# A language-model block in eight token blocks: where the FFN weights are split and turned, and in what order block 0 is attended

## What is computed

```python
h = rms_norm(rms_norm(emb[x], norm_weight) @ proj.T)            # [16*256, 512]
n = layernorm(h)
q, k = feature_map(n @ Wq.T) / sqrt(32), feature_map(n @ Wk.T)   # per head, width 32
attn = tril(q @ k.T) ** 2
h = h + ((attn @ (n @ Wv.T)) / (attn.sum(-1) + eps)) @ Wo.T
y = fwht(layernorm(h) * SU_ug)                                   # 512 wide
u = silu(y @ W_gate.T * s_g) * (y @ W_up.T * s_u)                # 2048 wide
out = h + (fwht(u * SU_dp) @ W_down.T) * s_d
```

## Time and profile before

| | us |
|---|---|
| time, median of 3 runs | 1403.45 (1400.7 to 1405.17) |
| the profiled execution | 1400.2 |
| its span in the trace | 1398.4 |
| prologue, to the first FFN matmul | 162.75 |
| block 0, gate and up slots | 154.75 |
| block 0, down slots | 55.0 |
| rest (block 1 to the end) | 1025.9 |

### The profile page before, as it was taken

One profiled execution on the slowest core, in us unless ns is written; L12 is line 12 of the kernel. 1 busy time (PEld: TensorE's weight loads), 2 busy tenths in 40 slices (PEclk: granted clock), 3 DMA queues, 4 the chain that ended last, 5 costly groups with the idle time before them and its releaser, 6 DMA issues.

```text
span 1398.4 us, 19203 instructions
## 1 busy us (share of the span) xinstructions
PE 1306.7 (93%) x7481; PEld 643.6 (46%) x7481; DVE 532.3 (38%) x1049; ACT 398.7 (29%) x703; POOL 422.9 (30%) x371
## 2 busy tenths in 40 slices
PE   5575598989999999999999999999999999999999
PEld 3352255554444444444444444444444444444444
DVE  1655567654422253226222432234222523251110
ACT  4453463440233113321233023311322123211220
POOL 0342143332144313432244213421433124321210
PEclk9888699999999999999999999999999999999999
DMA  8911100002100130003000210012001300020000
GB/s 297 288 27 23 24 1 9 8 8 54 53 8 9 31 75 8 15 15 80 19 16 8 68 38 8 15 42 64 8 8 23 83 8 15 15 68 23 0 0 30
DMA packets 101681, 55.73 MB, mean 40 GB/s; under 512 B 74180, under 2 KB 90872, under 8 KB 101112
## 3 DMA queue, kind: packets, MB, share of 16 engines
q1 hardware_dynamic: 98112, 45.77, 12.8%
q0 software_dynamic: 2560, 8.39, 2.0%
q10 hardware_dynamic: 952, 0.75, 0.2%
HBM read 29.47 MB, written 8.65 MB: 27 GB/s over the span
## 4 chain that ended last, share of the span: by engine, by line
PE 83%; DVE 6%; DMA 4%; ACT 4%; issue 2%; POOL 1%; SPq 0%; DVEq 0%; ACTq 0%
PE bank L1078 24%; PE bank L1079 24%; PE bank L1080 23%; DMA prod<-sg 3%; PE bank L1231 3%; PE bank L1073 2%; PE bank L1216 2%; PE bank L1215 2%; PE bank L1121 1%; DMA hid<-in_L_tok_norm_weight 1%; PE bank L1240 1%; ACT xT L855 1%; DVE wgu L477 1%; PE bank L1071 1%; ACT wgu L855 1%
## 5 line engine op out<-in xcount | busy, mean ns | idle before, releaser
L1078 PE MATMUL bank<-xT,wgu 128*128 128x512 f16 x1024 | 389.3, 380 | 1.4 <-DVE xT L708 1.4
L1079 PE MATMUL bank<-xT,wgu 128*128 128x512 f16 x1024 | 389.3, 380 | 0.0
L1080 PE MATMUL bank<-xT,wgu 128*128 128x512 f16 x1024 | 389.2, 380 | 0.0
L398 POOL TENSOR_TENSOR hid<-a,hid 128x512 f16<-128x512 f32 x128 | 147.9, 1156 | 512.0 <-ACT hid L855 512.0
L743 DVE SCALAR_TENSOR_TENSOR a<-bank,kap,sg 128x512 f32<-128x512 f32 x128 | 96.0, 750 | 477.5 <-PE bank L1080 324.4
L1078 PE MATMUL bank<-wd,hid 128*128 128x512 f16 x512 | 194.3, 379 | 0.0
L1079 PE MATMUL bank<-wd,hid 128*128 128x512 f16 x512 | 194.1, 379 | 0.0
L1080 PE MATMUL bank<-wd,hid 128*128 128x512 f16 x512 | 194.0, 379 | 0.0
L358 POOL TENSOR_TENSOR p<-prod,p 128x512 f16<-128x512 f32 x128 | 153.2, 1199 | 128.4 <-ACT p L855 128.4
L855 ACT ACTIVATE hid<-a 128x512 f16<-128x512 f32 x128 | 80.6, 630 | 279.5 <-DVE a L743 279.5
L1080 PEld LDWEIGHTS bank<-xT,wgu 128*128 128x128 f16 x1024 | 100.4, 98 | 121.6 <-issue 1.4
(11 more groups left out here) (178 smaller groups left out, 1245.8 us busy)
## 6 DMA issues: line engine op xcount, KB each, us to landing
out<-a SPq DMA_DIRECT2D x24, 256.0 KB, 2.2
wgu<-in_L_ffn_W_gate SPq DMA_DIRECT2D x16, 256.0 KB, 5.5
wgu<-in_L_ffn_W_up SPq DMA_DIRECT2D x16, 256.0 KB, 5.0
wd<-in_L_ffn_W_down SPq DMA_DIRECT2D x4, 1024.0 KB, 9.4
ids_b<-in_x SPq DMA_DIRECT2D x8, 256.0 KB, 3.5
out<-h_row SPq DMA_DIRECT2D x8, 256.0 KB, 2.0
xT<-in_L_tok_proj_weight SPq DMA_DIRECT2D x1, 1024.0 KB, 8.6
p<-in_L_attn_Wq SPq DMA_DIRECT2D x1, 1024.0 KB, 13.8
```

The costliest lines, as they stand in the source:

```text
L398: nc.gpsimd.tensor_tensor(hid[:, 1, s, :], a32[:, :], hid[:, 0, s, :], ALU.subtract)\
L1078: mm(dst, w[0], v[0], start=first, stop=False)
L1079: mm(dst, w[0], v[1], start=False, stop=False)
L1080: return mm(dst, w[1], v[0], start=False, stop=final)
```

## The change

1. **Loads.** The load of the norm weight is issued before that of the projection instead of after it. A group of four gate or up units comes with one DMA of 2 KB rows instead of four; the tile `wgu` has another layout.
2. **Gate and up units.** 12 units (0 to 11) are turned on PE in slots 1 to 12 of block 0's attention, with one diagonal per unit. The other 20 are prepared in slots 0 to 9 of block 0's FFN, two per slot, without PE: ACT scales the unit in place, ACT writes the f16 high part to a staging buffer (L966, twice), POOL the low part (L428), and SP turns the pair with a DMA transpose (L329) into `wgu`. There are three staging buffers (`RING`), taken in turn; the next user waits for the landing.
3. **W_down.** The 16 butterflies are two per slot in slots 2 to 9 (L566, L567). A unit is then split in SBUF (ACT L966, DVE L556), three per slot in slots 10 to 14 and one in slot 15, turned by a DMA transpose through the same three buffers, and multiplied with the f16 Hadamard matrix in the slot after (two f16 matmuls, L1256 and L1257: after the gate half, after the up half and after the attention step), then evicted (ACT L966, DVE L574).
4. **Block 0's attention** has 18 slots. The count and the W_v turns come earlier, the squares of W_o and of the units move between the slots, the low parts of `att` are made between the first products, and `p` alternates between two tiles. W_o is turned in slots 13 to 16. `oT` and `xT` are turned by PE (eight f16 transposes into a bank) and copied by one ACT instruction of 128x1024. The W_o rows are no longer slots but a `tail()`, in which bound, norm and scale steps stand between the rows on DVE.
5. **Banks.** Block 0's gate half alternates between two banks in slots 0 to 7; the up half has one.

Its core (lines of `...` are left out):

```diff
@@ -19,19 +19,18 @@
...
-BEFORE = 16
-UNITS_IN_SLOT = (0, 0) + (1,) * BEFORE + (0,) * 14
-UNITS_BESIDE = 16
-NORM_AT = {4: 1, 24: 2}
-SCALE_AT = {6: 1, 26: 2}
-DIAG_AT = {6: (2,), 10: (3,), 26: (4,), 27: (5,)}
-BOUND_AT = 17
-NORM_BESIDE, SCALE_BESIDE = 2, 3
-DIAG_BESIDE = {3: (6,), 5: (7,)}
-BOUND_BESIDE, FIT_BESIDE = 4, 5
+RING = 3
+TURNED = 12
+UNIT_AT = tuple(range(1, 13))
+UNITS_BESIDE = 10
+SQUARES_AT = {j: (3, j) for j in range(4)} | {8 + j: (4 + j // 4, j % 4) for j in range(8)}
+WO_SQUARES_AT = (4, 5, 6, 7)
+WO_UNIT_AT = (13, 14, 15, 16)
+DOWN_SQUARES = (3, 3, 3, 3, 2, 2)
+BOUND_BESIDE, FIT_BESIDE = 1, 6
+MIX_BESIDE = (2, 2, 3, 3, 4, 4, 5, 5, 6, 6, 7, 7, 8, 8, 9, 9)
+SPLIT_BESIDE = (10, 10, 10, 11, 11, 11, 12, 12, 12, 13, 13, 13, 14, 14, 14, 15)
 DOWN_ORDER = (3, 2, 0, 1)
-MIXED_BEFORE = 2
-MIX_BESIDE = (1, 2, 3, 4, 5, 6, 7, 8, 9, 10, 11, 12, 12, 13)
...
+HEADS_AT0 = (4, 8, 12, 16)
+O_AT0 = (5, 9, 13, 16)
+O_FLIP_AT0 = (6, 10, 14, 17)
+SLOTS0 = 18
...
+def down_third(s, i):
+    return down_splits(s - 1)[i:i + 1]
...
-        GATE0, UP0, D_TURN, D_HADA = banks[0], banks[1], banks[2], banks[3]
+        GATE0, UP0, D_HADA = [banks[0], banks[1]] * 4 + [banks[0]] * 8, banks[2], [banks[3], banks[1]]
...
             nc.sync.dma_start(late[:, 1536:1792], c_square).then_inc(S["c_land"], 16)
+            nc.sync.dma_start(nw_b, rows(norm_w, D)).then_inc(S["nw_land"], 16)
             nc.sync.dma_start(small_raw[0], quarters(proj_w)).then_inc(S["p_land"], 16)
-            nc.sync.dma_start(nw_b, rows(norm_w, D)).then_inc(S["nw_land"], 16)
...
                 w, g = (w_up if n % 2 else w_gate), n // 2
-                for i in range(4):
-                    rows_of_tile = w[512 * g + P * i:512 * g + P * i + P, :].rearrange("p (k d) -> p k d", k=DC)
-                    nc.sync.dma_start(raw[n][:, :, i, :], rows_of_tile).then_inc(S[f"gu_land{n}"], 16)
+                rows_of_tile = w[512 * g:512 * g + 512, :].rearrange("(i p) d -> p i d", p=P)
+                nc.sync.dma_start(raw[n], rows_of_tile).then_inc(S[f"gu_land{n}"], 16)
...
+            def unit_turn(x):
+                if x < UNITS:
+                    sp.wait_ge(S["st_low"], x - TURNED + 1)
+                else:
+                    sp.wait_ge(S["st_lo"], x - UNITS + TURNED + 1)
+                nc.sync.dma_start_transpose(unit_home(x), stage_of(x).rearrange("p l d -> p (l d)"))\
+                    .then_inc(turning(x), 16)
...
+                for x in units_beside(s) + [UNITS + v for v in down_splits(s)]:
+                    unit_turn(x)
+                if s in SUMS_AT:
+                    o_turn(1, SUMS_AT.index(s))
...
+            def unit_low(x):
+                pool.wait_ge(S["st_hi"], x + 1)
+                nc.gpsimd.tensor_tensor(stage_of(x)[:, 1, :], unit_raw(x), stage_of(x)[:, 0, :], ALU.subtract)\
+                    .then_inc(S["st_low"], 1)
...
             for s in range(SLOTS):
                 feed(0, s)
+                for x in units_beside(s):
+                    unit_low(x)
                 product(1, s)
...
+            def unit_low(x):
+                dve.wait_ge(S["st_hi"], x + 1)
...
+                else:
+                    nc.vector.scalar_tensor_tensor(stage_of(x)[:, 1, :], unit_raw(x), unit_scale(x), stage_of(x)[:, 0, :],
+                                                   ALU.mult, ALU.subtract).then_inc(S["st_lo"], 1)
...
+            def tail():
+                for m in range(4):
+                    row_sum(0, m)
+                    if m:
+                        x_low(0, m - 1)
+                    if m > 1:
+                        xT_low(0, m - 2)
+                    row_norm(0, m)
+                    if m == 0:
+                        pair_norm(2)
+                        half_terms(0)
+                    if m == 1:
+                        pair_scale(2)
+                        bound_low(0)
+                    if m == 2:
+                        half_scale(0)
+                    if m == 3:
+                        pair_norm(3)
+                xT_low(0, 2)
+                x_low(0, 3)
+                xT_low(0, 3)
+                pair_scale(3)
...
-                for u in units_beside(2 * s):
-                    unit(u, D_TURN)
-                for v in down_evicts(2 * s):
-                    down_unit(v)
                 feed(0, s, UP0)
-                for u in units_beside(2 * s + 1):
-                    unit(u, D_TURN)
-                for v in down_evicts(2 * s + 1):
+                for v in down_splits(s):
+                    unit_low(UNITS + v)
...
+                for v in down_third(s, 2):
+                    down_unit(v)
...
+            def unit_high(x):
+                if x < TURNED:
+                    n, i = unit_place(x)
+                    act.wait_ge(S["turned"], x + 1)
+                    copy(wgu[:, n, i, 0, :, :].rearrange("p k f -> p (k f)"), TURN[x % 3][:, :]).then_inc(S["st_hi"], 1)
+                    return
+                if x >= TURNED + RING:
+                    act.wait_ge(*landed(x - RING))
+                else:
+                    act.wait_ge(S["wo_ready"], 1)
+                if x < UNITS:
+                    act.wait_ge(S["gu_scaled"], x // 8 + 1)
+                    copy(unit_raw(x), unit_raw(x), scale=unit_scale(x)).then_inc(S["st_scaled"], 1)
+                    act.wait_ge(S["st_scaled"], x - TURNED + 1)
+                    copy(stage_of(x)[:, 0, :], unit_raw(x)).then_inc(S["st_hi"], 1)
+                else:
+                    act.wait_ge(S["d_mix"], 4 * ((x - UNITS) // 4) + 4)
+                    act.wait_ge(S["bound_done"], 1)
+                    copy(stage_of(x)[:, 0, :], unit_raw(x), scale=unit_scale(x)).then_inc(S["st_hi"], 1)
...
-            def down_turn(v):
-                dt, fq = DOWN_ORDER[v // 4], v % 4
+            def down_hada(v):
+                if v > 1:
+                    pe.wait_ge(S["d_lo"], v - 1)
                 if v == 0:
-                    pe.wait_ge(S["d_diag"], 1)
-                    pe.wait_ge(S["w_lo"], UNITS)
-                else:
-                    pe.wait_ge(S["d_copied"], v)
-                pe.wait_ge(S["d_mix"], 4 * (v // 4) + 4)
-                turn(D_TURN, lambda i: WD[dt][:, (4 * fq + i) * P:(4 * fq + i + 1) * P],
-                     lambda i: d_diag[:, dt, :], S["d_turned"])
-
-            def down_hada(v):
-                pe.wait_ge(S["d_copied"], v + 1)
-                if v:
-                    pe.wait_ge(S["d_lo"], v)
-                else:
                     pe.wait_ge(S["bound_low"], 3)
-                mm(D_HADA[:, :], hada, wt[:, v % 2, :], start=True, stop=True).then_inc(S["d_hada"], 1)
-
+                pe.wait_ge(*landed(UNITS + v))
+                w = wd[:, DOWN_ORDER[v // 4], v % 4, :, :, :].rearrange("p l f d -> p l (f d)")
+                mm(D_HADA[v % 2][:, :], hada16[:, :], w[:, 0, :], start=True, stop=False)
+                mm(D_HADA[v % 2][:, :], hada16[:, :], w[:, 1, :], start=False, stop=True).then_inc(S["d_hada"], 1)
...
+            def tail():
+                wo_rows(0, 0)
+                wo_rows(0, 1)
+                wo_rows(0, 2)
+                x_flip(0)
+                wo_rows(0, 3)
+                bound_sum(0)
+                for m in range(4):
+                    x_mix(0, m)
+                    if m < 3:
+                        x_flip(m + 1)
 
 
...
             for s in range(SLOTS):
                 if s < FT:
                     if s == 0:
                         pe.wait_ge(S["xT_done"], 4)
-                        pe.wait_ge(S["w_lo"], BEFORE)
-                        pe.wait_ge(S["bound_low"], 1)
-                    else:
-                        pe.wait_ge(S["silu_done"], s)
-                    if s % 4 == 0:
-                        pe.wait_ge(S["w_lo"], min(UNITS, 8 * (s // 4) + 8))
-                    feed_half(s, 0, GATE0, S["gate_ready"])
-                    for v in down_evicts(2 * s):
+                        pe.wait_ge(S["wo_lo"], 4)
+                    if s >= 2:
+                        pe.wait_ge(S["silu_done"], s - 1 if s < 9 else s)
+                    pe.wait_ge(*landed(2 * s))
+                    feed_half(s, 0, GATE0[s], S["gate_ready"])
+                    for v in down_third(s, 0):
                         down_hada(v)
-                    for u in units_beside(2 * s):
-                        turn_beside(u)
-                    for v in down_turns(2 * s):
-                        down_turn(v)
                     if s == BOUND_BESIDE + 1:
                         bound_sum(1)
                     if s == FIT_BESIDE + 1:
                         bound_sum(2)
                     if s:
                         pe.wait_ge(S["a_done"], s)
+                    pe.wait_ge(*landed(2 * s + 1))
                     feed_half(s, 1, UP0, S["up_ready"])
-                    for v in down_evicts(2 * s + 1):
+                    for v in down_third(s, 1):
                         down_hada(v)
```

(22 more changed lines are left out.)

790 lines of the change are left out of this document (428 added, 362 removed).

## The result

The changed kernel takes 1409.58 us (median; 1407.02 to 1410.50), the kernel before 1403.11 in the same comparison. The ratio is 1.0046 with a 95% interval of 1.0036 to 1.0056: slower by 6.5 us. The forecast was 1412, slower as well, within a range of 1378 to 1427. The profiled execution has a span of 1406.5 us, 8.1 more than before.

A forecast was written before the change was run, and what follows sets the result against it. A chain over all engines was taken to bound the prologue, PE the FFN slots. 1400.2 - 10.7 (prologue) + 19.2 (block 0's gate and up slots) = 1408.7 us profiled, 1412 on the median's scale; range 1378 to 1427.

The forecast's parts named there:

- First head sums: Prologue: the first head sums start at 63.4 us instead of 80.06, a gain of 16.7 us.
- the order of the loads: Start of the prologue: norm weight loaded before the projection gains 1.3 us, bounds 0 and a few us.
- the tail: End of the prologue, the W_o rows: 41 us instead of 36.10, a loss of 4.9 (bounds 34 and 45).
- both stalls: Tail: DVE waits at `bound_low(0)` for a PE sum and at `pair_norm(3)` for ACT's squares, 3 to 4 us each.
- The mechanism: Block 0 FFN, slots 2 to 9: DVE's butterflies and POOL's instructions take turns, 9.05 us a slot.
- a sign of being wrong: Block 0 FFN, slots 2 to 9: slots under 8 us would show the forecast wrong; it expected 9 us.
- the buffers as a rival: Three staging buffers make ACT wait for landings, deciding from 4.4 us a transpose: 1425 to 1435 us; with more lock, chance 0.11.
- The chain: Block 0 FFN, slots 11 to 15: one chain through every engine, 11.4 us a slot, 13.3 with half rate.
- half rate: Slots 11 to 15: PE at half rate for some 4 us after idling costs 1.9 us more per slot.
- the case that came: Whole kernel: slower by 5 to 16 us, 1408 to 1420 us, chance 0.45.
- the faster rival: Block 0 FFN: preparation hides, gate and up slots take 130 to 150 us, total 1375 to 1398; chance 0.30.
- The preparation hides: Block 0 FFN: turns cost less than taken, slots 2 to 9 take 6.4 to 7 us, total 1375 to 1398; chance 0.30.

The follow-up runs named there:

- e6: Changed kernel with the norm weight's load issued behind the projection's again: 1408.9 us, ratio to the kernel before 1.0049.
- e7: Changed kernel with the tail's bound_low(0), half_scale(0) and pair_norm(3) one step later on DVE: 1404.9 us, ratio to the kernel before 1.0026.
- e2: Changed kernel with each W_down butterfly made on one eighth of its columns, the rest left out: 1388.5 us, ratio to the kernel before 0.9890.
- e8: Changed kernel with the same 16 butterflies spread, one per slot in slots 2 to 9, two in 10 to 13: 1395.2 us, ratio to before 0.9953.
- e3: Changed kernel with DVE's first two W_down evictions of a slot before the three splits: 1396.4 us, ratio to the kernel before 0.9941.
- the combined kernel: Changed kernel with fourth staging buffer, evictions before splits, butterflies spread, tail's bound and norm steps a row later: 1375.0 us, ratio to before 0.9810.
- e1: Changed kernel with a fourth staging buffer for the gate and up units: 1405.6 us, ratio to the kernel before 1.0007.

## Why the prediction was right

**Prologue.** First head sums and first W_o matmul came within 1 us of the forecast. The 1.3 us for the order of the loads stay unproven (e6): the chain waits for the projection until 12.1 us, where before it waited for the norm weight until 12.3. The term that was mis-sized is the tail. It was taken as 41 us and was 37.6: both stalls exist and are on the path (e7), but I took 3 to 4 us for each and they are 2.2 and 2.6, one at `bound_low(0)` and one at `pair_norm(3)`, and taking both off the path gave 3.1 us:

```profile
128.35 0.16 DVE L579 TENSOR_SCALAR h<-bank 128x1 f32<-128x1 f32 x1 [2.20 <-PE bank L1247]
...
142.32 0.17 DVE L532 TENSOR_SCALAR h<-h 128x8 f32<-128x8 f32 x1 [2.63 <-ACT hid L963]
```

The tail's 3.4 us are the difference between a prologue gain of 10.7 and the 14.3 measured; the stalls explain some 2 of them, the rest is open.

**Slots 2 to 9.** The mechanism was there (the rows above, e2, e8), and `a` of slot 10, expected 104.6 us after the first gate matmul, ended at 101.1. The terms fit less well than this sum. Slots 0 and 1 took 13.7 us, not 17; the sum had three of four butterfly halves slow, and 18 of 32 were. The mean of slots 2 to 9 is 9.15 us, but slots 2, 3, 5, 6 and 9 are under 8 us, which the prediction had named as a sign of being wrong. That part of the agreement is luck. (Before, slots 2 to 9 took 8.8 us on average, not 9.3, and the prediction's terms up to slot 10 add up to 104.9; neither changes the forecast.) What the prediction did not see is that the loop through the three buffers has the same period. It named the buffers as a rival, but for W_down's slots, with a threshold of 4.4 us a transpose that is never reached; in the gate and up slots the loop runs through ACT and POOL's queue, and a transpose of 3.2 us is only a third of it. The miss cost little, because the higher of two equal limits was in the sum; it would have cost 10 us in a forecast of a version without the turns. The distribution was not right: slots 0 to 3 run at PE's pace (25.3 us), since the first turned unit is not needed before slot 6, and the wait is paid in slots 4 and 8 (17.0 and 13.8 us), where the heads wait 8.7 and 5.3 us for POOL, and in slots 7 and 10 (11.0 and 10.2 us).

**Slots 11 to 15.** The chain was forecast at 13.3 us a slot and takes 13.5 to 13.8; slot 11's up half was expected to end 113.3 us after the first gate matmul and ended at 113.0. e3 shows that the place of the evictions is the main cause: with them in front, slots 12 to 14 fall from 40.8 to 31.9 us, below the 32.5 of the kernel before. What half rate costs there was read from the spacing of the matmuls and not tested apart.

**The net.** Expected +19.2 and -10.7, measured +20.5 and -14.3, with +0.8 in the down slots and another 1.2 us spread over the rest of the trace, both of which were forecast at nothing: 8.1 in the profiled executions, 6.5 in the medians, against 8.5 forecast. The places were right; that the total came so close is partly luck, since a prologue that was 3.6 us better than forecast paid for the other three. The range, 1378 to 1427, reached from clearly faster to clearly slower, and only 0.45 stood on the case that came; its figure for the faster rival does not follow from its terms (FFN slots of 130 to 150 us give about 1368 to 1388, not 1375 to 1398). "The preparation hides" was wrong for this kernel, but the combined kernel comes near its number of 1375 by taking away the causes.

## What to carry to other kernels

Work taken from the busiest engine pays only as far as the engines that get it, and the order in their queues, can keep its pace: here PE's busy time in these slots fell by 22 us and the slots grew by 20. Count what a step queues behind: an eviction behind three splits, a low part behind another stream's instructions. Where two limits lie close together, an edit that lifts one of them can show almost nothing (e1); lift both, or stub one out, before an idea is dropped.
